# Second layer's router of blocks 0 to 3 computed jointly with weights held still, and its choice of experts four slots later

## The reference

```python
x = x + _L0_ffn_ref(_L0_cond_ref(x, cond_1024, ...), ...)
x = x + _L1_ffn_ref(_L1_cond_ref(x, cond_1024, ...), ...)
```

```python
def _L1_cond_ref(x, t_emb, W_router, router_bias, s_w1, s_w3, s_w2, r_w1, r_w2):
    for e in range(N_SHARED):                       # 2 shared experts
        h = silu(x_flat @ s_w1[e].T) * (x_flat @ s_w3[e].T)
        shared_out = shared_out + h @ s_w2[e].T
    router_in = concatenate([x_flat, t_flat], axis=-1)
    s = sigmoid(router_in @ W_router.T)             # 8 experts
    _, topk_idx = top_k(s + router_bias, 2)
    s_sel = take_along_axis(s, topk_idx, axis=1)
    gates = s_sel / (s_sel.sum(1) + 1e-9)
    for e in range(N_EXPERTS):                      # 8 routed experts
        h = gelu(x_flat @ r_w1[e].T)
        routed_out = routed_out + h @ r_w2[e].T * gates_full[:, e:e + 1]

def _L1_ffn_ref(x, U1, V1, b1, U2, V2, b2):         # low rank, 32
    return (gelu((x @ U1) @ V1 + b1) @ U2) @ V2 + b2
```

## Time and profile before

| | us |
|---|---|
| median of 3 runs | 890.34 |
| lowest and highest | 889.7, 891.0 |
| span of the profiled execution, first to last instruction | 886.9 |
| TensorE busy | 870.3 (98%) |
| VectorE busy | 682.8 (77%) |
| ACT busy | 574.0 (65%) |
| GpSimd busy | 402.0 (45%) |

### The profile page before, as it was taken

One profiled execution on the slowest core, in us unless ns is written; L12 is line 12 of the kernel. 1 busy time (PEld: TensorE's weight loads), 2 busy tenths in 40 slices (PEclk: granted clock), 3 DMA queues, 4 the chain that ended last, 5 costly groups with the idle time before them and its releaser, 6 DMA issues.

```text
span 886.9 us, 12606 instructions
## 1 busy us (share of the span) xinstructions
PE 870.3 (98%) x3838; PEld 690.2 (78%) x3838; DVE 682.8 (77%) x1094; ACT 574.0 (65%) x1029; POOL 402.0 (45%) x376
## 2 busy tenths in 40 slices
PE   8999999999999999999999999999999999999997
PEld 5788888777888888888888888888888777777773
DVE  7877777869689786686686686686665888998887
ACT  7888888765555455555555555555555678989895
POOL 7557783135356453253253252252232227754462
PEclk9999999999999999999999999999999999999999
DMA  9589981023113112012012012011010049582700
GB/s 311 211 276 313 293 295 35 1 86 135 48 48 111 42 42 84 4 45 84 1 48 83 1 48 84 0 48 48 1 48 0 1 108 209 106 178 53 161 25 36
DMA packets 36404, 83.23 MB, mean 94 GB/s; under 512 B 4464, under 2 KB 14320, under 8 KB 34544
## 3 DMA queue, kind: packets, MB, share of 16 engines
q1 hardware_dynamic: 36336, 82.42, 30.1%
HBM read 71.39 MB, written 6.83 MB: 88 GB/s over the span
## 4 chain that ended last, share of the span: by engine, by line
PE 76%; DVE 9%; issue 4%; ACT 3%; SPq 3%; DMA 2%; POOL 1%; DVEq 0%; ACTq 0%; POOLq 0%
PE ps L932 16%; PE ps L951 16%; PE ps L937 16%; PE ps L992 8%; PE ps L994 8%; PE ps L987 8%; DVE HL L1571 3%; SPq L658 1%; PE ps L974 1%; PE ps L972 1%; DVE Hf L1551 1%; DMA ST<-scratch 1%; DVE Hf L1558 1%; ACT HH L1084 1%; SPq L771 1%
## 5 line engine op out<-in xcount | busy, mean ns | idle before, releaser
L1078 ACT ACTIVATE Sg<-ps 128x512 f32<-128x512 f32 x288 | 171.7, 597 | 242.6 <-PE ps L951 242.3
L1551 DVE TENSOR_TENSOR Hf<-ps,Sg 128x512 f32<-128x512 f32 x288 | 197.9, 688 | 147.7 <-ACT Sg L1078 97.5
L1663 POOL TENSOR_TENSOR HL<-Hf,HH 128x512 fp32r<-128x512 f32 x130 | 174.2, 1347 | 157.4 <-ACT HH L1084 141.0
L1084 ACT ACTIVATE HH<-Hf 128x512 fp32r<-128x512 f32 x346 | 216.1, 625 | 21.1 <-DVE Hf L1551 14.4
L1571 DVE TENSOR_TENSOR HL<-Hf,HH 128x512 fp32r<-128x512 f32 x248 | 220.1, 888 | 4.3 <-ACT HH L1084 3.2
L932 PE MATMUL ps<-XHL,WBH 128*128 128x512 f32 x512 | 203.7, 398 | 1.8 <-DVE Hf L1551 1.8
L951 PE MATMUL ps<-XHL,WBH 128*128 128x512 f32 x512 | 202.2, 395 | 0.0
L937 PE MATMUL ps<-XHL,WBL 128*128 128x512 f32 x512 | 202.0, 395 | 0.0
L1678 POOL TENSOR_TENSOR XT<-XT,TMP 128x512 f32<-128x512 f32 x64 | 84.0, 1312 | 248.9 <-DVE TMP L1425 248.7
L932 PEld LDWEIGHTS ps<-XHL,WBH 128*128 128x128 f32 x512 | 96.0, 188 | 27.0 <-DVE Hf L1551 4.0
L951 PEld LDWEIGHTS ps<-XHL,WBH 128*128 128x128 f32 x512 | 96.0, 188 | 23.0
(11 more groups left out here) (275 smaller groups left out, 1327.6 us busy)
## 6 DMA issues: line engine op xcount, KB each, us to landing
CWB<-scratch SPq DMA_DIRECT2D x14, 1024.0 KB, 4.5
GWD<-expert_down SPq DMA_DIRECT2D x21, 576.5 KB, 4.4
GWU<-expert_up SPq DMA_DIRECT2D x21, 514.0 KB, 5.2
CWB<-scratch SPq DMA_DIRECT2D x40, 256.0 KB, 5.6
ST<-in_wb_dram SPq DMA_DIRECT2D x8, 768.0 KB, 6.2
ST<-scratch SPq DMA_DIRECT2D x24, 256.0 KB, 8.8
GX<-XT SPq DMA_DIRECT2D x68, 64.0 KB, 3.0
XT<-in_x_dram SPq DMA_DIRECT2D x8, 256.0 KB, 5.6
```

What stands on the lines that cost most here:

```text
L1078: e.activation(Sg[:, it.n % NG, :], zb[z % NZ][:, :], ACT.Silu).then_inc(s_act, 1)
L1084: e.activation(HH[:, it.n % NH, 0:it.cols], hidden_place(it), ACT.Copy).then_inc(s_hi_act, 1)
L1551: e.tensor_tensor(Hf[:, it.n % NS, :], zb[z % NZ][:, :], Sg[:, it.n % NG, :], ALU.mult).then_inc(s_prod, 1)
L1663: e.tensor_tensor(HL[:, it.n % NH, :], Hf[:, it.n % NS, :], HH[:, it.n % NH, :].bitcast(F32), ALU.subtract).then_inc(s_lo_pool, 1)
```

## The change

The router of blocks 0 to 3 uses the steps `four`, `four_copy`, `four_turn` and `four_logit` that blocks 4 to 7 had already. `four` gets a second key, the half (0 or 1), and a new entry `lag_b[3]: ("B", 0)`. `route_b`, `logit_b`, WR and its semaphore are gone. The slots of group 0's choice begin at `lag_b[3] + 5` instead of `lag_b[3] + 1`, and with them the slot of the copy to q3, from which `gate_slots` is computed.

```diff
-        WR = sb("WR", [P, 2, 8], F32R)
...
-        split_b, route_b, logit_b = when(t_b, 2), when(lag_b[:4]), when(lag_b[:4], 1)
-
-        four = {t_g + 16: "A", lag_b[7]: "B"}
+        split_b = when(t_b, 2)
+
+        four = {t_g + 16: ("A", 1), lag_b[3]: ("B", 0), lag_b[7]: ("B", 1)}
         four_copy = {t + 1: v for t, v in four.items()}
-        four_turn, four_logit = [{t + i + (v == "B"): v for t, v in four.items()} for i in (2, 3)]
+        four_turn, four_logit = [{t + i + (v[0] == "B"): v for t, v in four.items()} for i in (2, 3)]
...
-        pick = [[lag_b[3] + 1 + i for i in (0, 1, 2, 3, 5, 6, 7, 8, 10, 11)],
+        pick = [[lag_b[3] + 5 + i for i in (0, 1, 2, 3, 5, 6, 7, 8, 10, 11)],
                 [pos["S", 2, 0, 0].k + i for i in (0, 1, 2, 3, 4, 5, 6, 7, 9, 10)]]
...
-                if k in route_b:
-                    b = route_b[k]
-                    bk = ab_bank(("B", b))
-                    e.wait_ge(*ab_free(("B", b)))
-                    e.wait_ge(s_wr, 2)
-                    e.wait_ge(s_b_lo, b + 1)
-                    for t in range(4):
-                        c = slice(t * 16, t * 16 + 16)
-                        wr = WR[:, :, :].rearrange("p a e -> p (a e)")
-                        e.matmul(bk[:, c], XH[:, b, t * P:t * P + P], wr, start=True, stop=False)
-                        mm = e.matmul(bk[:, c], XL[:, b, t * P:t * P + P], wr, start=False, stop=True)
-                    mm.then_inc(s_small, 1)
                 if k in four:
-                    layer = four[k]
-                    bk = ab_bank((layer, "four", 1))
-                    e.wait_ge(*ab_free((layer, "four", 1)))
+                    layer, half = four[k]
+                    bk = ab_bank((layer, half, "four"))
+                    e.wait_ge(*ab_free((layer, half, "four")))
                     e.wait_ge(s_rz, 3 if layer == "A" else 5)
-                    e.wait_ge(s_a_hi if layer == "A" else s_b_hi, NBLK)
-                    e.wait_ge(s_a_lo if layer == "A" else s_b_lo, NBLK)
+                    e.wait_ge(s_a_hi if layer == "A" else s_b_hi, 4 * half + 4)
+                    e.wait_ge(s_a_lo if layer == "A" else s_b_lo, 4 * half + 4)
                     for q in range(4):
                         w = RZ[:, 0 if layer == "A" else 1, 96 - 32 * q:224 - 32 * q]
-                        e.matmul(bk[:, :], w, XH[:, 4 + q, :], start=q == 0, stop=False)
-                        mm = e.matmul(bk[:, :], w, XL[:, 4 + q, :], start=False, stop=q == 3)
+                        e.matmul(bk[:, :], w, XH[:, 4 * half + q, :], start=q == 0, stop=False)
+                        mm = e.matmul(bk[:, :], w, XL[:, 4 * half + q, :], start=False, stop=q == 3)
                     mm.then_inc(s_small, 1)
...
-                if k == text + 6:
-                    e.tensor_copy(WR[:, 0, :], S("wrx")).then_inc(s_wr, 1)
-                    e.wait_ge(s_wr, 1)
-                    e.tensor_tensor(WR[:, 1, :], S("wrx"), WR[:, 0, :].bitcast(F32), ALU.subtract).then_inc(s_wr, 1)
...
-                if k in logit_b:
-                    b = logit_b[k]
-                    e.wait_ge(*small.of(("B", b)))
-                    got = ab_bank(("B", b))[:, 0:64].rearrange("p (t a e) -> p t a e", a=2, e=8)
-                    link(e.tensor_tensor(LR[:, 4 * b:4 * b + 4, 0:8], got[:, :, 1, :], TP[:, 4 * b:4 * b + 4, :], ALU.add))
-                    after()
-                    e.tensor_tensor(LR[:, 4 * b:4 * b + 4, 0:8], got[:, :, 0, :], LR[:, 4 * b:4 * b + 4, 0:8],
-                                    ALU.add).then_inc(s_ab, 1)
```

More of the change, by code:

```diff
@@ L238, in build @@
         s_max = sem("s_max")
-        s_gw, s_wr = sem("s_gw"), sem("s_wr")
+        s_gw = sem("s_gw")
         s_rz, s_four = sem("s_rz"), sem("s_four")
@@ L458, in build @@
             for layer, route, logit, turn, turned in (("A", route_a, logit_a, turn_a, turned_a),
[L459 to L463, removed]
+                                                      ("B", {}, {}, turn_b, turned_b)):
+                if k in route:
                     for b in route[k]:
@@ L471, in build @@
                 if k in logit:
-                    ab_done.add((layer, 4 * logit[k] + 3 if layer == "A" else logit[k]))
+                    ab_done.add((layer, 4 * logit[k] + 3))
                 if k in turned:
@@ L476, in build @@
             if k in four:
-                ab_of[four[k], "four", 1] = len(ab_of)
-                small.add((four[k], "four"))
+                ab_of[four[k] + ("four",)] = len(ab_of)
+                small.add(four[k] + ("four",))
             if k in four_turn:
-                ab_of[four_turn[k], "logits", 1] = len(ab_of)
-                small.add((four_turn[k], "logits"))
+                ab_of[four_turn[k] + ("logits",)] = len(ab_of)
+                small.add(four_turn[k] + ("logits",))
             if k in four_logit:
-                ab_done.add((four_logit[k], 7))
+                layer, half = four_logit[k]
+                ab_done.add((layer, 4 * half + 3))
             if k in low_rank:
@@ L510, in ab_bank, with four_count @@
             return ab[ab_of[key] % 2]
+        def four_count(half):
+            return [("A", 1), ("B", 0), ("B", 1)].index(half) + 1
         def ab_free(key):
@@ L517, in ab_free @@
                 user = "B", "turn", 1
[L518 to L521, removed]
+            if user[2:3] == ("four",):
+                return s_four, four_count(user[:2])
+            if user[2:3] == ("logits",):
+                user = user[0], 4 * user[1] + 3
             if user[:2] == ("A", "half"):
@@ L864, in tensor_program @@
                     mm.then_inc(s_small, 1)
                 if k in four_turn:
-                    layer = four_turn[k]
-                    bk = ab_bank((layer, "logits", 1))
-                    e.wait_ge(*ab_free((layer, "logits", 1)))
-                    e.wait_ge(s_four, 1 if layer == "A" else 2)
+                    layer, half = four_turn[k]
+                    bk = ab_bank((layer, half, "logits"))
+                    e.wait_ge(*ab_free((layer, half, "logits")))
+                    e.wait_ge(s_four, four_count((layer, half)))
@@ L1031, in scalar_program @@
                 if k in four_copy:
-                    layer = four_copy[k]
-                    e.wait_ge(*small.of((layer, "four")))
-                    e.activation(CB[:, 0, :], ab_bank((layer, "four", 1))[:, :], ACT.Copy).then_inc(s_four, 1)
+                    layer, half = four_copy[k]
+                    e.wait_ge(*small.of((layer, half, "four")))
+                    e.activation(CB[:, 0, :], ab_bank((layer, half, "four"))[:, :], ACT.Copy).then_inc(s_four, 1)
                 if k in soft_b:
@@ L1456, in vector_program @@
                 if k in four_logit:
-                    layer = four_logit[k]
+                    layer, half = four_logit[k]
                     n = 16 if layer == "A" else 8
-                    e.wait_ge(*small.of((layer, "logits")))
-                    got = ab_bank((layer, "logits", 1))[:, :].rearrange("p (t q c) -> p q t c", t=4, q=4)
-                    out = LR[:, 16:32, 0:n].rearrange("p (q t) c -> p q t c", t=4)
+                    a = 16 * half
+                    e.wait_ge(*small.of((layer, half, "logits")))
+                    got = ab_bank((layer, half, "logits"))[:, :].rearrange("p (t q c) -> p q t c", t=4, q=4)
+                    out = LR[:, a:a + 16, 0:n].rearrange("p (q t) c -> p q t c", t=4)
                     low = got[:, :, :, n:2 * n]
@@ L1466, in vector_program @@
                     else:
-                        link(e.tensor_tensor(out, low, TP[:, 16:32, :].rearrange("p (q t) c -> p q t c", t=4), ALU.add))
+                        link(e.tensor_tensor(out, low, TP[:, a:a + 16, :].rearrange("p (q t) c -> p q t c", t=4), ALU.add))
                     after()
```

## The result

| | us |
|---|---|
| before, median of 4 runs | 890.67 |
| changed, median of 4 runs (896.72 to 899.2) | 897.84 |
| ratio, 95% interval | 1.0083 (1.0069 to 1.0098) |
| span of the profiled execution, changed | 894.9 (its time: 896.72) |

A forecast was written before the change was run, and what follows sets the result against it. TensorE was taken to bound the kernel, busy 870.3 of 886.9 us. The seventh gate of block 1, 7.3 + 1.5 = 8.8 us later, gives a span of 895.7, plus 3.4 outside: 899.1 us, range 893.5 to 902.5.

The forecast's parts named there:

- TensorE's sum: Router on TensorE: four matmul groups removed, 3.60 us; eight wide matmuls and four transposes added, 2.31; net 1.29 us saved.
- Its lead ahead of the joint router: TensorE, before the joint router of blocks 0 to 3: up to 2.7 us ahead of the kernel before.
- VectorE's run: VectorE's dense work from the choice to the copy to q3: starts 698.4, lasts 24.4 us, copy at 722.8, 7.3 later.
- TensorE's wait for q4: At the transpose of the gates: some 2 us instead of 1.25, hidden by what follows.
- First gate: First broadcast gate of block 0: lands at 728.2 us, against a use at 724.91 before.
- The loads: Broadcast gates up to block 1's seventh: 1.52 us each, slower than R slots of 1.16; the seventh lands at 751.1.
- the extra load ahead of block 1's: SP's queue: block 2's first gate is issued ahead of all of block 1's, costing one load, 1.52 us.
- The chain behind it: From block 1's seventh gate through HH, table loads, sigmoid and Sg to TensorE's start, 747.35 before: moves by 8.8 us.
- Outside the span: Time outside the profiled span: 890.34 - 886.9 = 3.4 us, added to the 895.7 us span.
- Rival 1: Gate loads under about 1.2 us each, so only the first gate's lateness of 3.3 us is lost: 893.6 us; chance 0.08.
- Rival 2: Not slower: R slots and z banks swallow the delay if gates take 0.94 us or less; 889.1 or 890 us; chance 0.06.
- Rival 3: TensorE's clock granted 1.2 GHz during waits in 16 R slots: 13 us more, some 912; chance 0.06, shared with another pile-up.

The follow-up runs named there:

- e2_order: Changed kernel with the first gate of block 2 put back behind block 1's eight in SP's order; 897.37 us, ratio 1.0078.
- e10_pairs_before: Kernel before, with one DMA loading an expert's gates for two blocks; 888.96 us, ratio 1.0001.
- e3_half: Changed kernel with gates of blocks 0 and 1 loaded into 64 of 128 partitions only; 891.23 us, ratio 1.0017.
- e8_width: Changed kernel with gates of blocks 0 and 1 loaded with 256 of 512 columns, all 128 partitions; 896.15 us in a single run.
- e9_pairs: Changed kernel with one DMA loading an expert's gates for two blocks, 128 descriptors of 4 KB; 896.20 us, ratio 1.0074.
- e11_pairs_dense: Changed kernel with the choice two slots earlier, no gap between its steps, and one DMA per expert for two blocks' gates; 891.76 us, ratio 1.0033.
- e6_dense: Changed kernel with blocks 0 to 3's transposes and logits one slot earlier, choice two slots earlier and without its one-slot gap; 892.23 us, ratio 1.0032.

## Why the prediction was right

899.1 us was forecast, 897.84 measured, and the path is the forecast one: a late copy, late gates that land more slowly than they are used, and a late S of block 2. Up to S the loss is 7.1 us where 8.8 was forecast. Step by step:

- **TensorE's sum**: 3.60 - 2.31 = 1.29. The added parts measured 1.85 and 0.43. Its lead ahead of the joint router was 2.55 against 2.7.
- **VectorE's run**: start at 698.4 forecast; the mark is 1.46 later in this trace, so 700.03 answers to 698.57. The copy at 723.76 answers to 722.3, forecast 722.8. The run was 23.7 us, not 24.4; I had left too much for the small steps. TensorE's wait for q4 was 1.68, forecast some 2.
- **First gate**: used at 728.1 by the same count, forecast 728.2. The copy came 0.5 earlier and the first load took 3.8 instead of 3.5.
- **The loads**: here lies the over-estimate. I had 15 loads at 1.52, 22.8 us; they took 21.3. The term that was mis-sized is the extra load ahead of block 1's: priced at 1.5, worth 0.6 in e2_order.
- **The chain behind it**: the two table loads, the sigmoid and the Sg followed as said, and TensorE started at 755.95 after 1.34 us of wait. But one sentence was too strong. I wrote that this chain from the gate already ended TensorE's wait in the kernel before. There the gate and the items' own pace met within 0.6 us, and e10_pairs_before shows that an earlier gate gains almost nothing. It did no harm to the forecast, because a later gate does bind. A landing time next to a use time doesn't tell which of the two waited.
- **Outside the span**: the 3.4 us were the median less the span of one execution; within the changed kernel's profiled execution it is 896.72 - 894.9 = 1.8. This does no harm, as the sum is then the median before plus 8.8. What has to be compared is the loss: 8.8 forecast, 7.2 by the medians. That 899.1 and 897.84 lie nearer to each other is luck: the kernel before came to 890.67 with its fourth run.
- **Rival 1** (loads fast enough) happened in e3_half, and cost less than its price: 1.3 us instead of 3.3. **Rival 2** put the point of no loss at 0.94 us a gate; at 0.79 there was still a loss of 0.17%, so that point was wrong: the first gate stays 2.2 us late, and the slots behind it took back only 0.3. **Rival 3**: the granted clock stayed at 1.00, its 2.4 GHz level, through the waits of up to 1.7 us.
- The Trainium skill's figure, 341 GB/s for 1 MB (DMA: Bandwidth & Descriptors, "Measured (HBM→SBUF, 128 partitions, SWDGE, issued from GpSimd)"), doesn't hold for these loads: at 256 KB in 1.42 us they run at 185 GB/s. The paired loads, 512 KB in 1.72, reach 305.

## What to carry to other kernels

When a step is moved down a hand-written order, follow it to the loads that hang on it, and ask two things: how far ahead of its first use the first one lands, and whether the row of them lands faster than it is used. Here a saving of 1.3 us on the busiest engine was paid for with 6.8 us of lateness of one small copy, and because the loads were slower than their users nothing took it back. A buffer that lands directly before its use may still not be what is waited for: make it land earlier and see whether anything moves. Look also at what else is placed by the slot that moves: a load of the next block slipped ahead of the current one.

## What the runs showed of the hardware

Up to 2 KB a descriptor, these broadcast loads from HBM cost by the number of their descriptors and hardly by their bytes; 4 KB added 0.2 to 0.5 us a load. Time from one load's landing to the next, with one queue:

| descriptors of a load | us a load |
|---|---|
| 64 of 2 KB (e3_half) | 0.79 |
| 128 of 1 KB (e8_width) | 1.36 |
| 128 of 2 KB (changed, e2_order, before) | 1.42, 1.47, 1.52 |
| 128 of 4 KB (e9_pairs, e11_pairs_dense) | 1.72, 1.94 |

With 128 descriptors of 2 KB on each of two queues it was 1.05 us a load or less. Whether this is so for any load from HBM, or only because all 128 descriptors read the same bytes, was not tried; nor was a load with fewer descriptors for as many partitions.

A second surprise is VectorE's operation of 16 elements a partition that took 1.27 us beside a GpSimd sum of 1.3 us, in the middle of the choice. VectorE's timeline in the changed kernel:

```profile
717.53 1.27 DVE L1373 TENSOR_SCALAR r<-r 128x16 f32<-128x16 f32 x1
```

GpSimd's timeline (POOL) in the changed kernel at the same time:

```profile
717.49 1.27 POOL L1656 TENSOR_TENSOR XT<-XT,TMP 128x512 f32<-128x512 f32 x1 [7.54 <-DVE TMP L1410]
```

It ends with the GpSimd operation, and others of its kind take 0.11 to 0.17 us. The same stood in the kernel before, so the change neither made nor removed it. That it is the company and not the operation, e6_dense shows, where no GpSimd operation runs at that moment (VectorE's timeline):

```profile
712.73 0.17 DVE L1373 TENSOR_SCALAR r<-r 128x16 f32<-128x16 f32 x1
```
